# The rounded part of the layer weights copied by ACT instead of POOL, in three pairs per sequence

## The reference

```
x = x + attn_a(layernorm(x))   # linear attention, 8 heads of 16, chunks of 64
x = x + ffn(layernorm(x))      # 6 layers: local attention (16 heads of 64) and gated MLP
x = x + attn_b(layernorm(x))   # retention with decay
x = x + ffn(layernorm(x))      # the same 6 layers again
```

## Time and profile before

| what | value |
|---|---|
| median of 3 runs | 3599.34 us |
| lowest and highest | 3585.8 and 3599.8 us |
| the profiled execution | 3594.74 us |
| its span in the trace | 3593.0 us |
| PE busy | 3163.0 us (88%) |
| DVE busy | 2902.4 us (81%) |
| ACT busy | 2277.0 us (63%) |
| POOL busy | 1805.2 us (50%) |

### The profile page before, as it was taken

How to read it: one execution, slowest core, us unless ns; L and a number is a source line. 1 busy time by engine, 2 the same in 40 slices (tenths; PEclk the granted TensorE clock), 3 DMA queues, 4 the chain that set the end, 5 groups by cost and what they waited for, 6 DMA issues and landing times. The chain is left out here.

```text
span 3593.0 us, 71552 instructions
## 1 busy us (share of the span) xinstructions
PE 3163.0 (88%) x25368; PEld 1992.0 (55%) x25560; DVE 2902.4 (81%) x2723; ACT 2277.0 (63%) x3693; POOL 1805.2 (50%) x823
## 2 busy tenths in 40 slices
PE   5769989989989989989956898998998998998996
PEld 3446656656655655656523565665665565565563
DVE  4559978978978978988924897897897997997995
ACT  1147766766766766767712676776776776776773
POOL 5435545545545545645500655554554554554551
PEclk8779999999999999999977999999999999999998
DMA  5444444454444444454411445545445445445442
GB/s 185 149 114 104 107 124 103 108 126 108 107 122 108 107 124 109 105 128 111 103 40 49 112 102 127 119 98 132 110 103 126 115 101 127 113 107 126 107 111 65
DMA packets 273778, 399.12 MB, mean 111 GB/s; under 512 B 75836, under 2 KB 104248, under 8 KB 273720
## 3 DMA queue, kind: packets, MB, share of 16 engines
q1 hardware_dynamic: 273720, 398.48, 45.1%
HBM read 66.34 MB, written 19.92 MB: 24 GB/s over the span
## 5 line engine op out<-in xcount | busy, mean ns | idle before, releaser
L920 POOL TENSOR_TENSOR f_u<-f_u 128x512 f32<-128x512 f32 x384 | 575.6, 1513 | 572.3 <-ACT f_u L806 572.3
L924 POOL TENSOR_TENSOR f_w<-f_w,f_ab 128x1024 f32<-128x1024 f32 x192 | 555.0, 2891 | 544.4 <-DVE f_w L961 544.4
L929 POOL TENSOR_TENSOR f_ab<-f_w,f_rn 128x1024 f32<-128x1024 f32 x192 | 589.0, 3068 | 334.0 <-DVE f_rn L971 323.6
L806 ACT ACTIVATE f_u<-ps 128x512 f32<-128x512 f32 x768 | 467.2, 608 | 270.7 <-PE ps L625 203.5
L961 DVE TENSOR_TENSOR f_w<-f_ab,f_tan 128x1024 f32<-128x1024 f32 x384 | 496.0, 1332 | 126.9 <-ACT f_ab L807 122.4
L623 PE MATMUL ps<-f_xh,f_wh 128*128 128x512 f32 x768 | 386.2, 503 | 214.8 <-DMA f_pa<-pa 137.8
L807 ACT ACTIVATE f_ab<-ps,f_pa 128x512 f32<-128x512 f32 x768 | 541.5, 705 | 1.2
L681 PE MATMUL ps<-f_tb,f_v 128*64 128x160 f32 (+1 forms) x6144 | 446.7, 299 | 18.1 <-DMA f_tb<-f_pt 16.9
L681 PEld LDWEIGHTS ps<-f_tb,f_v 128*64 128x64 f32 x6144 | 399.9, 138 | 108.7 <-issue 106.3
L818 ACT ACTIVATE ps<-ps 128x512 f32<-128x512 f32 x384 | 204.6, 573 | 360.6 <-PE ps L642 360.6
L660 PEld LDWEIGHTS ps<-f_kb,f_qb 128*32 128x32 f32 x12288 | 339.6, 114 | 155.0 <-issue 123.7
(11 more groups left out here) (169 smaller groups left out, 5037.6 us busy)
## 6 DMA issues: line engine op xcount, KB each, us to landing
f_kb<-f_ab SPq DMA_DIRECT2D x1536, 64.0 KB, 2.0
f_qb<-f_ab SPq DMA_DIRECT2D x768, 128.0 KB, 2.4
f_tb<-f_pt SPq DMA_DIRECT2D x1344, 64.0 KB, 2.0
f_wh<-split_w SPq DMA_DIRECT2D x48, 384.0 KB, 4.3
f_wl<-split_w SPq DMA_DIRECT2D x48, 384.0 KB, 4.4
a_w_raw<-wqkv SPq DMA_DIRECT2D x24, 384.0 KB, 4.0
split_w<-a_w_hi SPq DMA_DIRECT2D x24, 384.0 KB, 2.3
split_w<-a_w_lo SPq DMA_DIRECT2D x24, 384.0 KB, 2.8
```

The source lines that it names most:

```text
L806: nc.scalar.activation(u[:, i, :], bank("qk", g, i), ACT.Square).then_inc(sq_done.sem, 1)
L920: nc.gpsimd.tensor_tensor(u[:, 2 * i + 1, :], u[:, 2 * i, :], u[:, 2 * i + 1, :], ALU.add).then_inc(sq_sum[i].sem, 1)
L924: nc.gpsimd.tensor_tensor(w[:, 0:2, :], w[:, 0:2, :], ab[:, k % 2, 0:2, :], ALU.add).then_inc(q_sum.sem, 1)
L929: nc.gpsimd.tensor_tensor(ab[:, k % 2, 0:2, :], w[:, 0:2, :], rn[:, 0:1, :].broadcast_to([128, 2, N]), ALU.mult).then_inc(rope_q.sem, 1)
```

## The change

ACT makes the rounded part by a plain activation copy of the raw tile into `w_hi`, and POOL only subtracts; the zero tile is gone. A new helper `weights_hi(m)` waits, for each half j, for the stores of the pair before and for the raw tile, and copies. ACT calls it three times in each pass that begins a sequence: behind the square `sq` (m = 0), behind the copies of `vk` (m = 1) and behind `den` (m = 2). SP and POOL loop over the 4 sequences, with the three pairs of each written out inside. The order of SP's loads and stores stays the same. PAIRS is 6 * 4 / 2 / 4 = 3.

```diff
+                PAIRS = DEPTH * QUADS // 2 // B
+                raw_in, hi_done, lo_done = ([Signal(f"{n}{j}", per, PAIRS) for j in range(2)] for n, per in (("raw_in", 16), ("hi_done", 1), ("lo_done", 1)))
+                split_out = [Signal(f"split_out{j}", 32, PAIRS, ahead=1) for j in range(2)]
+                SPLIT_USES = [(PAIRS * per, (c - PAIRS) * per) for per in (1, 16, 32) for c in range(PAIRS + 1)]
-                ACT_USES = [(1, -1), (1, 0), (1, 1), (4, -4)]
+                ACT_USES = [(1, -1), (1, 0), (1, 1), (4, -4)] + SPLIT_USES
...
-                    with pool.Fori(0, DEPTH * QUADS // 2) as n:
-                        now = Steps(pool, n + 1, ((1, 0), (16, 0), (32, 0)))
-                        for j in range(2):
-                            pool.wait_ge(raw_in[j].sem, now.count(raw_in[j]))
-                            pool.wait_ge(split_out[j].sem, now.count(split_out[j], -1))
-                            nc.gpsimd.tensor_tensor(w_hi[:, j], w_raw[:, j], zero[:, :].broadcast_to([C, 6 * 128]), ALU.add).then_inc(hi_done[j].sem, 1)
-                            pool.wait_ge(hi_done[j].sem, now.count(hi_done[j]))
-                            nc.gpsimd.tensor_tensor(w_lo[:, j], w_raw[:, j], w_hi[:, j].bitcast(F32), ALU.subtract).then_inc(lo_done[j].sem, 1)
+                    with pool.Fori(0, B) as s:
+                        now = Steps(pool, s + 1, SPLIT_USES)
+                        for m in range(PAIRS):
+                            for j in range(2):
+                                pool.wait_ge(hi_done[j].sem, now.count(hi_done[j], m))
+                                nc.gpsimd.tensor_tensor(w_lo[:, j], w_raw[:, j], w_hi[:, j].bitcast(F32), ALU.subtract).then_inc(lo_done[j].sem, 1)
...
+                        def weights_hi(m):
+                            for j in range(2):
+
+                                act.wait_ge(split_out[j].sem, now.count(split_out[j], m - 1))
+                                act.wait_ge(raw_in[j].sem, now.count(raw_in[j], m))
+                                nc.scalar.activation(w_hi[:, j], w_raw[:, j], ACT.Copy).then_inc(hi_done[j].sem, 1)
+
                         if cur:
                             act.wait_ge(S["xc"].sem, now.count(S["xc"]))
                             nc.scalar.activation(sq[:, :], xc[:, :], ACT.Square).then_inc(S["sq"].sem, 1)
+                            weights_hi(0)
                             act.wait_ge(S["var"].sem, now.count(S["var"]))
...
                                 nc.scalar.activation(vk[:, 2 * i:2 * i + 2, :], ps[:, 3 + i, :].rearrange("p (t n) -> p t n", t=2), ACT.Copy).then_inc(S["vk_sb"].sem, 1)
+                            weights_hi(1)
...
                             nc.scalar.activation(den[:, :], ps[:, 1, 0:TILES * AH], ACT.Abs).then_inc(S["den1"].sem, 1)
+                            weights_hi(2)
```

More of the change, by code:

```diff
@@ L82, in stage_a @@
                 causal, nw, ident = t("causal", [128, 128]), t("nw", [C, 1]), t("ident", [128, 128])
-                w_raw, zero = t("w_raw", [C, 2, 6 * 128]), t("zero", [C, 1])
+                w_raw = t("w_raw", [C, 2, 6 * 128])
                 w_hi, w_lo = t("w_hi", [C, 2, 6 * 128], F32R), t("w_lo", [C, 2, 6 * 128], F32R)
@@ L98, in stage_a @@
                 s_tile, st_tile, o_tile = (Signal("a_" + n, 1, TILES) for n in ("s_tile", "st_tile", "o_tile"))
-                raw_in, hi_done, lo_done = ([Signal(f"{n}{j}", per) for j in range(2)] for n, per in (("raw_in", 16), ("hi_done", 1), ("lo_done", 1)))
-                split_out = [Signal(f"split_out{j}", 32, ahead=1) for j in range(2)]
+                PAIRS = DEPTH * QUADS // 2 // B
+                raw_in, hi_done, lo_done = ([Signal(f"{n}{j}", per, PAIRS) for j in range(2)] for n, per in (("raw_in", 16), ("hi_done", 1), ("lo_done", 1)))
+                split_out = [Signal(f"split_out{j}", 32, PAIRS, ahead=1) for j in range(2)]
+                SPLIT_USES = [(PAIRS * per, (c - PAIRS) * per) for per in (1, 16, 32) for c in range(PAIRS + 1)]
                 PE_USES = [(1, c) for c in range(-1, 1)] + [(2, -2), (2, 0), (4, -4)] + [(4, c) for c in range(-7, -3)]
-                ACT_USES = [(1, -1), (1, 0), (1, 1), (4, -4)]
+                ACT_USES = [(1, -1), (1, 0), (1, 1), (4, -4)] + SPLIT_USES
                 DVE_USES = [(1, -1), (1, 0), (1, 1), (2, 0)] + [(4, c) for c in range(-7, -3)]
@@ L125, in _ @@
                         sp.sem_inc(split_out[j].sem, 32)
-                    with sp.Fori(0, DEPTH * QUADS // 2) as n:
-                        now = Steps(sp, n + 1, ((1, 0), (16, 0), (32, 0)))
-                        for j in range(2):
[L129 to L133, removed]
+                    with sp.Fori(0, B) as s:
+                        now = Steps(sp, s + 1, SPLIT_USES)
+                        for m in range(PAIRS):
+                            for j in range(2):
+                                row = bass.ds(s * (2 * PAIRS) + 2 * m + j, 1)
+                                sp.dma_start(w_raw[:, j], wf["wqkv"][row].rearrange("l c n -> (l c) n")).then_inc(raw_in[j].sem, 16)
+                            for j in range(2):
+                                row = bass.ds(s * (2 * PAIRS) + 2 * m + j, 1)
+                                sp.wait_ge(lo_done[j].sem, now.count(lo_done[j], m))
+                                for part, w in enumerate((w_hi, w_lo)):
+                                    sp.dma_start(split_w[row, part].rearrange("l c n -> (l c) n"), w[:, j].bitcast(F32)).then_inc(split_out[j].sem, 16)
                     for j in range(2):
@@ L138, in _ @@
                 def _(pool):
-                    cleared = sem("a_cleared", scope)
-                    nc.gpsimd.memset(zero[:, :], 0.0).then_inc(cleared, 1)
-                    pool.wait_ge(cleared, 1)
-                    with pool.Fori(0, DEPTH * QUADS // 2) as n:
-                        now = Steps(pool, n + 1, ((1, 0), (16, 0), (32, 0)))
-                        for j in range(2):
-                            pool.wait_ge(raw_in[j].sem, now.count(raw_in[j]))
-                            pool.wait_ge(split_out[j].sem, now.count(split_out[j], -1))
-                            nc.gpsimd.tensor_tensor(w_hi[:, j], w_raw[:, j], zero[:, :].broadcast_to([C, 6 * 128]), ALU.add).then_inc(hi_done[j].sem, 1)
-                            pool.wait_ge(hi_done[j].sem, now.count(hi_done[j]))
-                            nc.gpsimd.tensor_tensor(w_lo[:, j], w_raw[:, j], w_hi[:, j].bitcast(F32), ALU.subtract).then_inc(lo_done[j].sem, 1)
+                    with pool.Fori(0, B) as s:
+                        now = Steps(pool, s + 1, SPLIT_USES)
+                        for m in range(PAIRS):
+                            for j in range(2):
+                                pool.wait_ge(hi_done[j].sem, now.count(hi_done[j], m))
+                                nc.gpsimd.tensor_tensor(w_lo[:, j], w_raw[:, j], w_hi[:, j].bitcast(F32), ALU.subtract).then_inc(lo_done[j].sem, 1)
                 @block.tensor
```

## The result

The changed kernel takes 3614.81 us in the median of 9 runs (3604.88 to 3621.34), the one before 3598.5 (9 runs, 3585.8 to 3600.08): a ratio of 1.0051 (95% interval 1.0036 to 1.0066). A second measurement gave 3611.4 against 3597.37 us, ratio 1.0041 (1.0025 to 1.0056). The change makes the kernel 0.4 to 0.5% slower. The forecast was 3604 us, a little slower.

The account below looks back on a forecast made before the run. The first stage (205.5 us) was taken as bound by a chain of waits, not an engine. Terms 0.7 + 6.1 + 1.5 gave +8.3 us: 3603.0 on the profiled time, 3607.6 on the median, 3604 taken; range 3589 to 3620.

Parts of the forecast that it names:

- Pair 2, behind `den`: Loop passes: ACT waits for raw weights with `oT` queued behind; +1.9, +3.1 and +1.1 us, together 6.1.
- disturbance: POOL's subtractions running against DVE's `qm`: 0.5 us taken per pass, +1.5 us in all.
- The 14.5 us from `vk` to `xb`: Loop passes: 9.8 round trip, 1.85 pair 2, 0.69 `oT`, 0.1 signals, 2.08 `wo` product.
- First part of pass 1: Pair 0 comes at 46.1 us and holds Ln, taking back DVE's first-pass gain: +0.7 us (-0.3 to +2).
- Other stretches of the stage: Rest of the first stage: copies fit under ACT's waits or what follows, costing nothing.
- The whole: Sum over the first stage, 0.7 + 6.1 + 1.5: +8.3 us, the stage ending near 213 us instead of 205.
- The rest of the kernel: The 3387.5 us behind the first stage cost nothing; a move larger than the stage's would show the forecast wrong.
- The quieter port wins: Rival: short hold at `den`, DVE sets the middle part; -11 us, 3584 us; chance 0.12.
- Hidden: Rival: round trip 2 us shorter, holds end with DVE's own work; within 3 us of before, 3596; chance 0.20.
- The long round trip: Rival: 3.1 us more per round trip, plus 3.2 for PE's lower clock; +22.4 us, 3617; chance 0.08.
- My line that `qm`'s median would stay above 1.21 us: Sign in the changed kernel's profile: DVE's `qm` product stays over 1.21 us in the median.
- The estimate from the Trainium skill, "DMA: Bandwidth & Descriptors": Raw weights' landing: 2.9 us against the trace's 4.0, making three holds each 1.1 us shorter, the result 3.3 lower.

Follow-up runs that it names:

- the second profiles: Both kernels profiled once more, nothing altered: first stage 207.6 us for the kernel before, 219.6 us for the changed kernel.
- The two other versions that were timed: Changed kernel with all pairs at other places on ACT, ratio 0.9959; with own tiles, raw loads together and all pairs behind Exp, ratio 0.9956.
- The run with early loads: Changed kernel with own tiles for each pair and six raw tiles loaded at the start of a pass: stage 211.8 us, single execution 3605.83 us.
- the quiet-port run: Kernel before with POOL's add and subtraction cut to 8 of 768 columns: stage 187.6 us, single execution 3578.5 us.

## Why the prediction was right, and where its sizes were off

The mechanism was right in the main: ACT holds at pair 2 for a round trip, `oT` queues behind it, and the quieter port goes unused. The direction and the range held, and "faster" never came near. The terms:

- **Pair 2, behind `den`: forecast 1.9 + 3.1 + 1.1, and 1.5 for disturbance, 7.6 us; measured 2.6 + 4.1 + 1.8, 8.5.** The 14.5 us from `vk` to `xb` were 15.2 to 15.5. Copies (0.842 us in the median), landing (4.2 against 4.0) and `oT` came as worked out. The two subtractions of pair 1 took 4.68 us and not 3.62 where they fell on DVE's products, which made the round trip 10.7 to 10.9 us instead of 9.8; I had charged 0.5 a pass for all disturbance. Against the second profiles the three passes lost 10.1 us.
- **First part of pass 1: forecast +0.7, measured +3.5 to 3.9.** This is the step that failed. I had the hold of pair 0 and `xn`'s collision with the subtraction (2.00 us), but pair 0 came at 47.2 us and not at 46.1: from the end of the subtractions it took 6.35 us and not 5.35, SP's last issues lying 0.95 us apart between two passes (41.03, 41.97, 42.93) and 0.5 within one (73.09, 73.61, 74.14). The projections started at 52.3 where I allowed up to 51.6. And there I ended the sum. PE, idle for 4.19 us, then ran part of them at the lower clock (granted 0.67, where the kernel before has 1.00), 1.8 us more up to the `qk` copies.
- **Other stretches of the stage: forecast 0, measured within 1 us each.** DVE's gain in the first pass came (PE's mean product of pass 1 at 35.2 us instead of 37.1), as did its loss to the hold.
- **The whole: forecast +8.3, stage +11.8 and +12.0, kernel +16.3 and +14.0 between medians (+18.4 and +14.8 by the ratios).** The two other versions that were timed moved with their stage (-13.4 and -15.1; -15.9 and -15.7). For the changed kernel 11.8 us lie just below the first interval (13.0 to 23.8 us), and 12.0 inside the second (9.0 to 20.1).
- **The rest of the kernel: forecast 0, not confirmed.** I had named it as a sign of being wrong if the rest moved by more than the stage. In the profiles it did: from 3387.5 to 3399.5 us, +12.0 against the stage's +11.8, and +14.2 in the second pair. The profiled executions of the changed kernel were slower than its medians and those of the kernel before faster, and by the medians the rest grew by 4.5 and 2.0 us only. But the changed kernel's ffn sums were the highest in both profiles. Whether anything behind the first stage is slower, by clock or otherwise, and why, stays open.

**The rivals.** *The quieter port wins* was priced at -11 us, on the condition that the raw weights come early. The run with early loads met that condition with ACT's places unchanged, and its stage was 211.8 us, still longer than before. So the condition was not enough: the subtractions have to leave DVE's products too. With both, the gain was 13 to 16 us. *Hidden* needed a shorter round trip; it was longer. *The long round trip* had PE's clock in it, at 3.2 us; the clock did play, in one pass, for 1.8. My line that `qm`'s median would stay above 1.21 us was a wrong sign to look for: it went to 1.212, with the slowest still 2.84, and it stands at 1.213 in one profile of the kernel before.

The estimate from the Trainium skill, "DMA: Bandwidth & Descriptors", section "Anatomy of one DMA", would have made each hold 1.1 us shorter; the holds were longer than forecast, so the trace's landing time was the better guide. What the Trainium skill, "GPSIMD Engine Reference", section "Specifications", says of contention with DVE instructions that have two SBUF inputs agrees with the quiet-port run, where `qm` fell to 1.218 us and the masks, which read PSUM, stayed at 1.22.

## What to carry to other kernels

A copy given to an engine with 170 us to spare still costs what is queued behind it, when it waits for a round trip and the engine runs in order. Before placing it, set the length of its round trip (all legs, stores too) against the distance between the places, and choose places inside waits that are there anyway: the same 24 copies made the stage 12 us longer in one set of places and 13 us shorter in another. When a hold goes, look what it had kept apart.

## What the hardware showed that I had not expected

POOL and DVE seem to take turns by whole operations: a scan of 1.22 us took 2.60 to 2.73 when it met a subtraction of 1.80, and the product with `ss` (0.68 us) took 2.29 in each loop pass of the changed kernel, while the `qm` beside it stayed at 1.21. In the kernel before one subtraction ran from 106.83 to 108.63 us; the scan that started at 107.12 ended at 109.72, 1.1 us behind it. So one badly timed operation of POOL's cost DVE 1.4 to 1.6 us of its 1.80. The stage of one unchanged kernel came out at 205.6 and 207.6 us, the difference lying mostly in its last pass (41.8 and 44.4).
